# A hybrid Mamba and attention block on one core: skip term moved to VectorE, attention a row later, MLP ended a row sooner

## The reference, cut to what matters

```python
xn = rmsnorm(x)                                    # per position over channels
fwd = mamba(xn); bwd = flip(mamba(flip(xn)))       # same weights, both directions
# mamba: u, z = split(in_proj(xn)); u = silu(causal conv of 4 taps(u))
#        dt, B, C = split(x_proj(u)); delta = softplus(dt_proj(dt))
#        h = exp(delta*A)*h + (delta*u)*B          # 16 states, along 1024 tokens
#        y = sum over states of h*C, + u*D_param   # u*D_param is the skip term
#        out_proj(y * silu(z))
x = x + res_scale * ((fwd + bwd) * scale_mod + sigmoid(depthwise 3x3(xn)) * xn)
t = x as tokens
t = t + attention(layernorm(t))                    # 6 heads of 64, causal, 1024 tokens
t = t + mlp(layernorm(t))                          # 384 -> 1536 -> gelu -> 384
```

## Time and profile before

| | |
|---|---|
| median of 3 runs | 4229.28 us (4217.98 to 4236.39) |
| the profiled execution | 4223.39 us, of which the span of instructions is 4221.6 us |
| DVE busy | 3587.6 us, 85% |
| PE busy | 3382.0 us, 80% |
| POOL busy | 2733.4 us, 65% |
| ACT busy | 2560.3 us, 61% |
| mean granted clock of PE | 0.877 |
| first scan of sample 0, last scan of sample 7 | 111.6 us, 3885.8 us |

### The profile page before, as it was taken

One profiled execution on the slowest core, in us unless ns is written; L12 is line 12 of the kernel. 1 busy time (PEld: TensorE's weight loads), 2 busy tenths in 40 slices (PEclk: granted clock), 3 DMA queues, 4 the chain that ended last, 5 costly groups with the idle time before them and its releaser, 6 DMA issues.

```text
span 4221.6 us, 40649 instructions
## 1 busy us (share of the span) xinstructions
PE 3382.0 (80%) x11610; PEld 1701.1 (40%) x11626; DVE 3587.6 (85%) x2721; ACT 2560.3 (61%) x3547; POOL 2733.4 (65%) x1692
## 2 busy tenths in 40 slices
PE   6503398978898798978889788988989789976997
PEld 2201145623364234732356233742356233641472
DVE  4999898998899998998989988999989998898121
ACT  3533557766675656756676666757667576765362
POOL 2888676676766767676766767667766777676000
PEclk9756699988999899988999899988999889997998
DMA  3999798887978889787978879888988889788000
GB/s 81 232 229 239 189 225 185 208 201 191 216 187 204 208 196 211 182 208 181 238 180 220 190 193 221 189 196 193 222 190 195 202 200 219 178 208 207 6 7 15
DMA packets 224024, 785.11 MB, mean 186 GB/s; under 512 B 25292, under 2 KB 40958, under 8 KB 223518
## 3 DMA queue, kind: packets, MB, share of 16 engines
q0 software_dynamic: 117504, 427.87, 52.4%
q1 hardware_dynamic: 106270, 354.32, 25.6%
HBM read 339.60 MB, written 39.85 MB: 90 GB/s over the span
## 4 chain that ended last, share of the span: by engine, by line
PE 35%; DVE 25%; issue 13%; DMA 11%; POOL 8%; ACT 7%; DVEq 0%; SPq 0%; ACTq 0%; POOLq 0%
DVE pB L1198 17%; PE pW L668 9%; PE pW L585 9%; DMA y<-hb 7%; POOL hb L1375 6%; PE pW L473 4%; DMA y<-area 3%; PE pW L516 3%; PE pW L601 2%; ACT pt L1002 2%; PE pW L735 2%; DVE hb L1207 2%; PE pW L550 2%; POOL y L1386 1%; DVE pB L1163 1%
## 5 line engine op out<-in xcount | busy, mean ns | idle before, releaser
L1198 DVE TENSOR_TENSOR_SCAN pB<-pB,hb 128x1024 f32<-128x1024 f32 x768 | 1757.0, 2288 | 40.2 <-POOL hb L1375 20.1
L1386 POOL DMA_DIRECT2D y<-hb x768 | 747.3, 973 | 736.6 <-DVE hb L1207 627.6
L1375 POOL TENSOR_TENSOR hb<-du_f,b_row 128x1024 f32<-128x1024 f32 x384 | 1036.8, 2710 | 131.9 <-DMA b_row<-bc_rows 108.3
L1375 POOL TENSOR_TENSOR hb<-uc_b,b_row 128x1024 f32<-128x1024 f32 x384 | 995.3, 2593 | 61.8 <-DMA y<-hb 60.2
L1207 DVE TENSOR_TENSOR hb<-pB,c_row 128x1024 f32<-128x1024 f32 x768 | 940.4, 1224 | 44.3
L821 ACT ACTIVATE pB<-delta,vec 128x1024 f32<-128x1024 f32 x384 | 428.8, 1117 | 383.7 <-DVE hb L1207 383.3
L821 ACT ACTIVATE pB<-xres,vec 128x1024 f32<-128x1024 f32 x384 | 429.1, 1119 | 325.7 <-DVE hb L1207 325.0
L668 PE MATMUL pW<-area,pt 128*128 128x64 f32 x3456 | 432.6, 279 | 20.0 <-ACT pt L1002 12.4
L668 PEld LDWEIGHTS pW<-area,pt 128*128 128x128 f32 x3456 | 405.0, 193 | 69.8 <-ACT pt L1002 59.7
L1242 DVE TENSOR_REDUCE stat<-pW 128x1 f32<-128x640 f32 (+7 forms) x361 | 258.7, 753 | 163.4 <-PE pW L588 163.4
L492 PE MATMUL pW<-area,xn_area 128*128 128x512 f32 x576 | 265.4, 616 | 41.5 <-DVE area L1285 27.0
(11 more groups left out here) (172 smaller groups left out, 4890.7 us busy)
## 6 DMA issues: line engine op xcount, KB each, us to landing
y<-hb POOLq DMA_DIRECT2D x768, 512.0 KB, 7.2
b_row<-bc_rows SPq DMA_DIRECT2D x256, 512.0 KB, 5.8
c_row<-bc_rows SPq DMA_DIRECT2D x256, 512.0 KB, 5.5
du_f<-in_x SPq DMA_DIRECT2D x8, 1536.0 KB, 13.6
kept_residual<-in_x SPq DMA_DIRECT2D x8, 1536.0 KB, 13.0
y<-area POOLq DMA_DIRECT2D x24, 512.0 KB, 8.0
xres<-kept_residual SPq DMA_DIRECT2D x8, 1536.0 KB, 10.5
out_x<-xa SPq DMA_DIRECT2D x8, 1536.0 KB, 6.8
```

The source lines that it names most:

```text
L1198: dve.tensor_tensor_scan(flow(d, buf), flow(d, buf), flow(d, hb[r % NHB][:, :]), 0.0, ALU.mult, ALU.add).then_inc(scan_done, 1)
L1375: pool.tensor_tensor(hb[r % NHB][:, :], du[d][:, k, :], b_row[g % 2][:, :], ALU.mult)\
L1386: pool.dma_start(y[:, k, :], hb[r % NHB][:, :], accum_op=ALU.add).then_inc(y_in[k], 16)
```

## The change

The skip term of the backward direction leaves ACT and POOL: in rows 21, 19 and 20 (`SKIP`, by tile) DVE multiplies by C in place in PSUM and then computes u*D + that in a second instruction. The three skip DMAs, their ACT passes and the waits on them are gone. Softplus steps and projections are placed anew. Attention runs from row 34 to 61 (was 33 to 60). `wo` runs in rows 63 and 64, in another order of tiles and banks, each item waiting only for the evacuations that it needs; `wo_add` is three each in rows 64 and 65. The second layernorm, `next_in`, `next_up` and the MLP move one row or two up; the MLP's last addition is in row 94. `narrow_copies` copies B and C first and the step-size rows second; `step_size` waits for both. DVE has all iterations written out. The three `kept` DMAs of POOL are issued between its first rows, no longer ahead of them.

```diff
-SKIP = (24, 27, 30)
+SKIP = (21, 19, 20)
-BEHIND = ([("step_silu", 0, 17), ("step_x", 0, 19)] + [("step_skip", k, 18 + k) for k in range(KT)]
-          + [(kind, k, (22, 26, 29)[k] + i) for k in range(KT)
+BEHIND = ([("step_silu", 0, 17), ("step_x", 0, 19)] + []
+          + [(kind, k, (22, 25, 28)[k] + i) for k in range(KT)
-S0, S1 = 33, 62
-PROJ = (15, 16, 17, 18, 19, 21, 22, 22, 23, 24, 24, 25, 26, 26, 27, 28, 29, 30, 31, 31)
+S0, S1 = 34, 62
+PROJ = (15, 16, 17, 18, 19, 20, 21, 22, 23, 24, 25, 26, 26, 27, 28, 29, 30, 31, 32, 32)
-    + [("ctx_t", t, S1 + t // 3) for t in range(6)] + [("wo", t, S1 + 2 + t // 3) for t in range(6)]
-    + [("wo_add", t, S1 + 3 + t // 2) for t in range(6)]
+    + [("ctx_t", t, S1 + t // 3) for t in range(6)] + [("wo", t, S1 + 1 + t // 3) for t in range(6)]
+    + [("wo_add", t, S1 + 2 + t // 3) for t in range(6)]
-    + norm(1, S1 + 5, S1 + 7, S1 + 8, S1 + 10, S1 + 11)
-    + [("next_in", t, S1 + (7, 10, 13)[t // 2]) for t in range(6)] + [("next_up", t, S1 + (8, 11, 14)[t // 2]) for t in range(6)]
-    + [("mlp_in", 0, S1 + 12), ("mlp_cast", 0, S1 + 13), ("mlp_split", 0, S1 + 14)] + mlp(0, S1 + 14) + mlp(1, S1 + 24), key=lambda x: x[2])
+    + norm(1, S1 + 4, S1 + 6, S1 + 7, S1 + 9, S1 + 10)
+    + [("next_in", t, S1 + (7, 9, 11)[t // 2]) for t in range(6)] + [("next_up", t, S1 + (8, 10, 12)[t // 2]) for t in range(6)]
+    + [("mlp_in", 0, S1 + 11), ("mlp_cast", 0, S1 + 12), ("mlp_split", 0, S1 + 13)] + mlp(0, S1 + 13) + mlp(1, S1 + 23), key=lambda x: x[2])
...
-                sp.wait_ge(xd_evac, at(4, b, 2 * d + 2))
+                sp.wait_ge(xd_evac, at(4, b, 2 * d + 1))
...
-                pe.wait_ge(xd_evac, at(4, b, (1, 1, 2, 4, 4, 4)[g]))
+                pe.wait_ge(xd_evac, at(4, b, 2 * d + 2))
...
-                    pe.wait_ge(ct_evac, at(6, a, 6))
-                    if n >= 4:
+                    if n < 4:
+                        pe.wait_ge(ct_evac, at(6, a, n + 3))
+                    else:
                         pe.wait_ge(wo_add, at(6, a, n - 3))
-                    project(pW[:, n % 4, :], o_w, slice(128 * m, 128 * m + 128), ctxT,
+                    project(out_bank(n), o_w, slice(128 * m, 128 * m + 128), ctxT,
...
-                    pe.wait_ge(wo_add, at(6, b - 1, 4))
+                    pe.wait_ge(wo_add, at(6, b - 1, 6))
...
+                act.copy(bc_raw[d], bank[0:32, :]).then_inc(xd_evac, 1)
                 act.copy(dtr[d][0:RANK, :], bank[32:56, :]).then_inc(xd_evac, 1)
-                act.copy(bc_raw[d], bank[0:32, :]).then_inc(xd_evac, 1)
...
-                    if n >= 14 and n % 2 == 0 and not alone(b):
-                        k = n // 2 - 7
-                        act.wait_ge(y_in[k], at(YIN, b, 16 * ((SKIP[k] - LAG - k) // KT + 2)))
...
+                if r == SKIP[k]:
+                    dve.tensor_tensor(pBC[r % 2][:, :], pBC[r % 2][:, :], c_row[g % 2][:, :], ALU.mult)\
+                       .then_inc(skip_step, 1)
+                    dve.wait_ge(uc1_ready, at(3, b, 3))
+                    dve.wait_ge(skip_step, at(KT, b, sorted(SKIP).index(r) + 1))
+                    dve.scalar_tensor_tensor(out=hb[r % NHB][:, :], in0=uc[1][:, k, :], scalar=vec[:, k, V_D:V_D + 1],
+                                             in1=pBC[r % 2][:, :], op0=ALU.mult, op1=ALU.add).then_inc(m2_done, 1)
...
-            samples(dve, iteration)
+            for b in range(NB + 1):
+                iteration(b, b < NB, b > 0, b < NB - 1)
...
+            def keep_local(b, k):
+
+                pool.wait_ge(loc_ready, at(KT, b, k + 1))
+                pool.dma_start(kept[b][128 * k:128 * k + 128, :], gate[k], accum_op=ALU.add).then_inc(kept_add[k], 16)
...
+                        if r < KT:
+                            keep_local(b, (1, 0, 2)[r])
...
-                        if r in SKIP:
-                            sum_skip(b, SKIP.index(r))
```

More of the change, by code:

```diff
@@ L39 @@
 NHB = 5
-YIN = 16 * (2 * NS + 1)
+YIN = 16 * 2 * NS
 LAG = 2
@@ L186, in hybrid_block @@
         uc = [uc_f, uc_b]
-        skip_row = [area1[:, k * L:(k + 1) * L] for k in range(KT)]
         du = [du_f, uc_b]
@@ L230, in hybrid_block @@
             sem(n) for n in ("dt_ready", "sum_ready", "sp_abs", "sp_exp", "sp_ready", "delta_ready", "du_ready"))
+        skip_step = sem("skip_step")
         da_ready, m1_done, scan_done, m2_done = (
@@ L319, in landed @@
         def landed(r):
-            return 16 * (r // KT + 1 + (r > SKIP[r % KT] - LAG))
+            return 16 * (r // KT + 1)
         def flow(d, ap):
@@ L672, in item @@
                 elif kind == "ctx_t":
-                    m, c = n // 2, n % 2
+                    m, c = n % KT, n // KT
                     pe.wait_ge(ctx_ready, at(NG, a, NG))
@@ L887, in tap_row_of, with skip @@
                                        scale=w).then_inc(tap_ready, 1)
-            def skip(b, d, k):
-                dcol = vec[:, k, V_D:V_D + 1]
-                if d == 0:
-                    act.wait_ge(uc_ready, at(6, b, 2 * k + 2))
-                    act.wait_ge(yz_ready, at(3, b, 0))
-                    act.activation(y[:, k, :], uc[0][:, k, :], ACT.Identity, scale=dcol).then_inc(yd_ready, 1)
-                else:
-                    act.wait_ge(uc1_ready, at(3, b, 3))
-                    act.wait_ge(cv_ready, at(12, b, 12))
-                    act.activation(skip_row[k], uc[1][:, k, :], ACT.Identity, scale=dcol).then_inc(yd_ready, 1)
+            def skip(b, k):
+                act.wait_ge(uc_ready, at(6, b, 2 * k + 2))
+                act.wait_ge(yz_ready, at(3, b, 0))
+                act.activation(y[:, k, :], uc[0][:, k, :], ACT.Identity, scale=vec[:, k, V_D:V_D + 1])\
+                   .then_inc(yd_ready, 1)
             def copy_u(b, t):
@@ L929, in item @@
                 if kind == "step_y" and not early:
-                    skip(b, 0, n)
+                    skip(b, n)
                 elif kind == "step_z" and not early:
@@ L938, in item @@
                     act.preload_act_table_set(LOG_EXP)
-                elif kind == "step_skip" and not early:
-                    skip(b, 1, n)
                 elif kind == "step_bc" and early:
@@ L1077, in iteration @@
                     for k in range(2):
-                        skip(b, 0, k)
+                        skip(b, k)
                     for r, d, n, k in rows():
@@ L1140, in times_u1 @@
                 dve.wait_ge(sum_ready, at(3, b, k + 1))
-                dve.wait_ge(yd_ready, at(6, b, 6))
+                dve.wait_ge(m2_done, at(ROWS, b, SKIP[k] + 1))
                 dve.tensor_tensor(du[1][:, k, :], dt_bank[KT + k][:, :], uc[1][:, k, :], ALU.mult).then_inc(du_ready, 1)
@@ L1206, in output_row @@
                 dve.wait_ge(scan_done, at(ROWS, b, r + 1))
-                dve.tensor_tensor(hb[r % NHB][:, :], pBC[r % 2][:, :], c_row[g % 2][:, :], ALU.mult)\
-                   .then_inc(m2_done, 1)
+                if r == SKIP[k]:
[5 more added lines that the diff above has]
+                                             in1=pBC[r % 2][:, :], op0=ALU.mult, op1=ALU.add).then_inc(m2_done, 1)
+                else:
+                    dve.tensor_tensor(hb[r % NHB][:, :], pBC[r % 2][:, :], c_row[g % 2][:, :], ALU.mult)\
+                       .then_inc(m2_done, 1)
             def item(kind, n, b, early):
@@ L1254, in item @@
                 elif kind == "wo_add" and not early:
-                    t, m, c = n, n // 2, n % 2
+                    t, m, c = n, n % KT, n // KT
                     toks = slice(c * HALF, (c + 1) * HALF)
                     dve.wait_ge(wo_ready, at(6, a, t + 1))
-                    dve.scalar_tensor_tensor(out=xa[:, m, toks], in0=pW[:, t % 4, :], scalar=vec[:, m, V_BO:V_BO + 1],
+                    dve.scalar_tensor_tensor(out=xa[:, m, toks], in0=out_bank(t), scalar=vec[:, m, V_BO:V_BO + 1],
                                              in1=xa[:, m, toks], op0=ALU.add, op1=ALU.add).then_inc(wo_add, 1)
@@ L1382, in sum_row @@
                 if r < KT:
-                    pool.wait_ge(yd_ready, at(6, b, 3))
+                    pool.wait_ge(yd_ready, at(3, b, 3))
                 else:
@@ L1386, in sum_row @@
                 pool.dma_start(y[:, k, :], hb[r % NHB][:, :], accum_op=ALU.add).then_inc(y_in[k], 16)
-            def sum_skip(b, k):
-                pool.wait_ge(yd_ready, at(6, b, 4 + k))
-                pool.wait_ge(y_in[k], at(YIN, b, 16 * ((SKIP[k] - LAG - k) // KT + 1)))
-                pool.dma_start(y[:, k, :], skip_row[k], accum_op=ALU.add).then_inc(y_in[k], 16)
             def iteration(b, layer0, layer1, more):
@@ L1397, in iteration @@
                     pool.wait_ge(kept_set, at(16, b, 16))
-                    for k in range(KT):
-                        pool.wait_ge(loc_ready, at(3, b, k + 1))
-                        pool.dma_start(kept[b][128 * k:128 * k + 128, :], gate[k], accum_op=ALU.add)\
-                            .then_inc(kept_add[k], 16)
                     for r in range(ROWS):
```

2 lines of the change are left out of this document (1 added, 1 removed).

## The result

The changed kernel takes 4326.08 us (median of 4 runs, 4325.59 to 4337.55) against 4225.86 us for the kernel before beside it: ratio 1.0242, 95% interval 1.0213 to 1.0271. It is slower, as forecast, but by 100 us and not by 60 (medians): 4283 was forecast, and the range ended at 4308. The profiled execution took 4325.63 us, its span is 4323.8 us (before 4221.6), so 102.2 us more; mean granted clock of PE 0.869 (before 0.877).

The account below looks back on a forecast made before the run. DVE, busy 85% of the span, was taken to bound the kernel. Six middle samples at +8.2 us (+49), sample 7 +9.8 and sample 0 +1 made +60 on 4223.39: 4283 us, range 4238 to 4308.

Parts of the forecast that it names:

- five stretches: Per middle sample: skip +3.7, softplus -5.1, wo and norm +4.0, ln_var ahead of next_in +2.1, boundary +3.5 us.
- Boundary: Row 94 to the next first scan: transfers issued earlier delay the last y DMA; +3.5 us, bounds -1.2 and +6.0.
- 38.0 + 0.9 behind `silu_u` 0: Boundary: first scan 38.0 us after silu_u 0, as in sample 0, plus 0.9 for the exchanged narrow copies.
- Softplus: Softplus steps in the rows: DVE's waits fall from 9.5 to 4.4 us (tiles 1.3, 1.7, 1.4); -5.1 a middle sample.
- `ln_var`: Rows after 69: PE takes ln_var before next_in, so decay 72 comes late; +2.1 us, bounds 0 and 4.
- Skip: Rows 19 to 21: three more DVE instructions of 1.23 us with nothing to hide them; +3.7 us a sample.
- `wo`: Additions wait 6.3 us for PE, the next norm's 2.30 us wait goes; net +4.0, bounds 0 and +5.5.
- Ends: Samples 7 and 0, outside the six middle ones: +9.8 us for sample 7, +1 for sample 0.
- the unslowed DMA: Rival at the boundary: y DMA not slowed, boundary loses 4.7 us a time; 4251 us in all, chance 0.14.
- The free ACT: Rival: softplus chain always ahead of DVE (-9.5), boundary keeps the branch's 2.85 us (-2.9); 4207 us, chance 0.10.
- PE sooner at `wo`: Rival at wo: PE a row sooner, so the six waits vanish, 6.3 us x 7; 4239 us, chance 0.08.
- the case I gave 0.08: Something worse: every y DMA landing at 12.5 us beside later waits in the rows; 4300 to 4315 us, chance 0.08.

Follow-up runs that it names:

- e1: Changed kernel with SP's three transfers (xa store, xres load, kept copy) held until row 95's y DMA has landed: 4260.37 us, 1.0091 of the kernel before.
- e12: Changed kernel with only the xres load and the copy to kept held until row 95's y DMA has landed: 4257.05 us, 1.0079 of the kernel before.
- e6: Changed kernel with projection 12 moved from row 26 to row 27: 4304.10 us, 1.0186 of the kernel before.
- e3: Changed kernel with the second layernorm's ln_var back in row 70, behind next_in 0 and 1: 4300.70 us, 1.0194 of the kernel before.
- e4: Changed kernel without the three added DVE instructions a sample, leaving out the backward skip term: 4285.11 us, 1.0158 of the kernel before.
- e5: Kernel before with DVE's iterations written out instead of looped: 4222.33 us, 0.9996 of the kernel before.

## Why the prediction was wrong

Every mechanism named is in the trace, and each of the five stretches that were to change has the sign forecast; sizes failed, and one cost was not in the sum at all. Per middle sample 16.4 instead of 8.2:

- **Boundary, +3.2: the step "I take a landing 10 us after row 95's product, between 5.3 and 12.5, nearer to sample 0".** It was 13.7 in all the middle boundaries, beyond the end I called upper. That end came from sample 0, where two of the transfers run, and I used it for a boundary with three, having counted three in the same paragraph; then I took less still. e1 shows what holding the transfers gives back (7.2 to 10.3), e12 that the two of sample 0 make nearly all of it. The other part of the step, 38.0 + 0.9 behind `silu_u` 0, held: 39.1. The packet rule that I cited from the Trainium skill, DMA: Bandwidth & Descriptors, section Queues, rings and completion order (Arbitration), would give about 10 us by my estimate; the trace says 13.7, and the measurement decides.
- **Softplus, +2.8 with attention: the step "For tile 1 two copies stand ahead of the passes: 1.7".** I counted the copies and took PE as ready for them. It was not: 4.55 us idle, granted clock 0.50 and then 0.67, copies 3.26 us late. e6 took 2.6 out. Tiles 0 and 2 came out at their sums, and the rest of the stretch 0.5 better.
- **`ln_var`, +2.0: "`ln_var` and `next_in` 5.3 to 5.5 us each".** Durations from rows at a high clock, put behind idle time that the change itself creates: 7.69 us after 9.08 us idle. e3 has 7.49 for the other one that comes first. The result lies at the upper bound of 4, 4.1.
- **Skip, +0.5:** the skip instruction takes 1.28 us and not 1.23, the pair starts 1.33 us apart, and a row grows by 1.40 us, in 24 places (e4).
- **`wo`, +0.2, right in part by luck:** the waits have the form worked out, but they bring only 2.2 us in the mean of samples 2 to 5 (5.2 of new waits, less 3.0 before). Another 1.8 are the norm's instructions, 5.7 us for 3.9 before: ending the wait moved them beside POOL's product, a cost that the sum put at nothing. The sixth item was ready nearly when forecast because two errors met: `wo` started 0.9 us later against DVE's rows, and PE took 2.61 us an item (15.65 for six), not 2.83 (which should have read 17.14/6 = 2.86).
- **Ends:** sample 7 cost 9.2 (3.2 in its rows and 6.0 behind them) against 9.8, and that agreement is luck: its `wo` and the rows behind it lost 0.9 and not 6.3, `out_project` started 7.8 us later and not 6.0, its y DMA landing 10.3 us after the product (forecast about 8), and the rest, which was to save 1, took 1.3 more, less than the same code varies by from run to run (e4). Sample 0 gained 3.1 where I had a loss of 1: POOL, rid of three DMAs, gave back 5.4 in rows 26 to 32 and 3.7 in rows 33 to 69 (forecast 4.5 in all; 2.5 of the 3.7 are the norm's instructions, 8.2 us before and 5.7 after), against 4.2 for the skip and 1.8 at its boundary, which had two of the three transfers beside its DMA before.

The rivals: the unslowed DMA is refuted by 13.7 us, and by e1, which is what that rival would have looked like. The free ACT is refuted in the boundary by e5, and in the softplus steps by the 56.9 us that DVE still waits there. PE sooner at `wo` is refuted by the four waits. What came nearest is the case I gave 0.08, "every y DMA landing at 12.5 beside later waits in the rows", and it too ended short, at 4315.

The three larger misses go the same way, and the norm with them: a landing, a copy, twelve matmuls and three instructions of DVE were each taken at the size that they have when nothing stands in their way.

## What to carry to other kernels

When a step is finished sooner, list what is queued behind it on the queues that issue transfers and what those will run beside: here 66 of 100 us hung on three transfers that used to start 4 us behind the last product and now start 3.4 us before its end. The mend is a wait that restores the old order, not the old place of the step. And when a change puts idle time ahead of PE's work, size that work by a row that follows idle time.
